# Gated delta rule: block-row sweeps written in place, four heads in four 32-column strips, and a new slot order

## What is computed

```
q, k, v = silu(conv4(x @ W))         # 128 channels a head, causal depthwise convolution of 4 taps
a, b    = sigmoid(x @ Wa + ba), sigmoid(x @ Wb + bb)
for t in range(256):
    err = S @ k_t - v_t
    S   = a_t * S - b_t * outer(err, k_t)
    o_t = S @ q_t
out = (layernorm(o) * sigmoid(x @ Wg)) @ Wo
```

## Time and profile before

| | |
|---|---|
| median of 3 runs | 3551.97 us (3543.28 to 3555.49) |
| profiled execution, its own time | 3545.73 us |
| span of its instructions | 3543.7 us |
| PE / DVE / ACT / POOL busy in the span | 89% / 70% / 53% / 52% |
| slots 10 to 63 | about us 1042 to 3060 of the span |
| draining slots and the second routed layer | from us 3094 |

### The profile page before, as it was taken

How to read it: one execution, slowest core, us unless ns; L and a number is a source line. 1 busy time by engine, 2 the same in 40 slices (tenths; PEclk the granted TensorE clock), 3 DMA queues, 4 the chain that set the end, 5 groups by cost and what they waited for, 6 DMA issues and landing times.

```text
span 3543.7 us, 68472 instructions
## 1 busy us (share of the span) xinstructions
PE 3137.7 (89%) x19888; PEld 2721.2 (77%) x19888; DVE 2494.0 (70%) x5733; ACT 1894.1 (53%) x3788; POOL 1829.4 (52%) x1918
## 2 busy tenths in 40 slices
PE   5999999646679999999999999999999999876773
PEld 3777777524469999899899899989989999766762
DVE  4565556565467778778777777777777777677766
ACT  2555555324356666666566566666656666433421
POOL 1111111133666767667576676766767676564332
PEclk9999999867799999999999999999999999988985
DMA  2000000023466565665656556566565665423211
GB/s 87 1 0 0 0 0 0 3 71 104 122 186 183 162 173 169 170 178 163 175 154 183 171 153 196 138 183 182 156 179 160 176 178 161 138 76 90 80 31 48
DMA packets 572226, 423.68 MB, mean 120 GB/s; under 512 B 228692, under 2 KB 475220, under 8 KB 571735
## 3 DMA queue, kind: packets, MB, share of 16 engines
q1 hardware_dynamic: 571862, 419.51, 41.6%
HBM read 276.39 MB, written 143.01 MB: 118 GB/s over the span
## 4 chain that ended last, share of the span: by engine, by line
PE 76%; DVE 13%; issue 4%; ACT 4%; POOL 3%; DMA 1%; DVEq 0%; SPq 0%; ACTq 0%; POOLq 0%
PE bank L1820 23%; PE bank L1871 22%; PE bank L1851 6%; PE bank L1955 5%; PE bank L1670 4%; PE bank L1645 3%; PE bank L1583 3%; PE bank L1655 2%; DVE dec L1427 1%; DVE acc L1418 1%; PE bank L1859 1%; POOL acc L740 1%; PE bank L1640 1%; ACT acc L972 1%; PE bank L1945 1%
## 5 line engine op out<-in xcount | busy, mean ns | idle before, releaser
L740 POOL TENSOR_TENSOR acc<-acc,shifted 128x510 f32<-128x510 f32 x384 | 611.2, 1594 | 448.6 <-DVE acc L1418 441.5
L1418 DVE SCALAR_TENSOR_TENSOR acc<-bank,conv_w,acc 128x254 f32<-128x254 f32 (+1 forms) x1536 | 631.0, 473 | 177.5 <-ACT acc L972 176.9
L970 ACT ACTIVATE shifted<-bank,conv_w 128x255 f32<-128x255 f32 x768 | 362.9, 472 | 435.4 <-PE bank L1820 310.7
L1820 PE MATMUL bank<-x_k,w_kq 128*128 128x256 f32 x2048 | 489.7, 384 | 41.9 <-DVE acc L1418 16.5
L1820 PEld LDWEIGHTS bank<-x_k,w_kq 128*128 128x128 f32 x2048 | 374.9, 192 | 92.1 <-issue 30.0
L972 ACT ACTIVATE acc<-bank,conv_b,conv_w 128x256 f32<-128x256 f32 x768 | 433.9, 565 | 0.0
L1871 PE MATMUL bank<-y,GT 128*128 128x128 f32 x2048 | 285.2, 284 | 56.5 <-DVE y L1458 56.5
L1871 PEld LDWEIGHTS bank<-y,GT 128*128 128x128 f32 x2048 | 269.9, 200 | 64.6 <-DVE y L1458 58.5
L1851 PE MATMUL bank<-kq 128*128 128x256 f32 x1024 | 276.1, 409 | 37.3 <-ACT kq L982 30.8
L767 POOL TENSOR_TENSOR ors<-ovar,half_neg 128x8 f32<-128x8 f32 x64 | 163.4, 2554 | 264.1 <-DVE ovar L1493 264.0
L757 POOL TENSOR_TENSOR inv<-inv,outer 128x30 f32<-128x30 f32 (+14 forms) x480 | 277.2, 578 | 37.6
(11 more groups left out here) (237 smaller groups left out, 6779.3 us busy)
## 6 DMA issues: line engine op xcount, KB each, us to landing
abc<-decay_scratch SPq DMA_DIRECT2D x64, 512.0 KB, 4.2
q_scratch<-kq SPq DMA_DIRECT2D x64, 512.0 KB, 3.8
M_scratch<-LM SPq DMA_DIRECT2D x64, 512.0 KB, 3.6
L_scratch<-LM SPq DMA_DIRECT2D x64, 512.0 KB, 4.8
LTm<-L_scratch SPq DMA_DIRECT2D x64, 512.0 KB, 4.1
MTm<-M_scratch SPq DMA_DIRECT2D x128, 256.0 KB, 3.6
kqm<-q_scratch SPq DMA_DIRECT2D x64, 512.0 KB, 4.2
k_scratch<-knw SPq DMA_DIRECT2D x64, 258.0 KB, 4.7
```

Of the source, the lines that this page charges most:

```text
L740: pool.tensor_tensor(dst, dst, shifted[:, u % 2, :, 1:], ALU.add).then_inc(Z["sumk" if u < 4 else "sumv"], 1)
L970: act.activation(shifted[:, u % 2, i % 2, 1:], pj[:, 0:SEQ - 1], ACT.Copy, scale=conv_w[:, kind, bass.ds(head, 1), TAPS - 2:TAPS - 1].rear ...
L1418: dve.scalar_tensor_tensor(out=acc[:, kind, i, t:], in0=pj[:, 0:SEQ - t], scalar=wcol, in1=acc[:, kind, i, t:], op0=ALU.mult, op1=ALU.add) ...
L1820: mm = pe.matmul(dst[:, i * SEQ:(i + 1) * SEQ], w[:, k, head * DK:(head + 1) * DK], x[:, k, :], start=(k == 0), stop=(k == CT - 1))
```

## The change

1. `GT` is filled once with identity matrices. `off_blocks` on DVE no longer multiplies by a mask but copies, for q = 32, 64, 96, the rows above block q into the block column q of `GT` (three copies of 32, 64 and 96 partitions x 4 heads x 32). The mask `above` is gone.
2. A sweep computes only block row k+1: `block_row` issues one matmul per head with a weight of 128x32 (the columns of that block of `GT`) and writes head i to partitions 32i to 32i+31 of the bank, so the four heads use the four 32-column strips of the PE array. Because of the identity in `GT` the product is already the finished row. It is copied in place into `vn` or `r1`: DVE copies heads 0 and 1, ACT copies heads 2 and 3 (32x128 each), and the next sweep waits for both (`y0` and `z0`, `y1` and `z1`). `y0`, `y1` are gone; the updates read `vn`, `r1`.
3. The order of the calls in a slot is new on all five engines, and two uses in `RING` change places. On DVE, `second_rhs` now stands before `decays` and `products`. On SP, `store_n` now stands before nine other transfers instead of last. On ACT, `silu(0)` stands before `tap(3)`.
4. In the preparation two pairs of store semaphores are merged, which changes no order.

The preparation on GpSimd:

```diff
+            pool.tensor_copy(GT[:].rearrange("p c h t -> p (c h t)"), id_many[:].rearrange("p n t -> p (n t)")).then_inc(Z["cons"], 1)
```

ScalarE's half of a sweep, new (`second_sweep` alike, with `r1`, `ap1`, `z1`):

```diff
+                def first_sweep(k):
+                    act.wait_ge(Z["ap0"], past(3 * h + k + 1))
+                    q = (k + 1) * BLK
+                    for i in range(HG // 2, HG):
+                        ins = act.copy(vn[hp][q:q + BLK, 0, i], bank[3][i * BLK:(i + 1) * BLK, 0:DK])
+                    ins.then_inc(Z["z0"], 1)
```

VectorE:

```diff
-                    dve.tensor_tensor(GT[:, tc], above[:].unsqueeze(1).broadcast_to([P, HG, P]), bank[3 + tc][:].rearrange("p (h t) -> p h t", h=HG),
-                                      ALU.mult).then_inc(Z["Gev"], 1)
+                    product = bank[3 + tc][:].rearrange("p (h t) -> p h t", h=HG)
+                    for q in range(BLK, P, BLK):
+                        ins = dve.tensor_copy(GT[0:q, tc, :, q:q + BLK], product[0:q, :, q:q + BLK])
+                    ins.then_inc(Z["Gev"], 1)
...
-                    dve.tensor_tensor(y0[:], vn[hp][:, 0], bank[3][:].rearrange("p (h v) -> p h v", h=HG), ALU.add).then_inc(Z["y0"], 1)
+                    q = (k + 1) * BLK
+                    for i in range(HG // 2):
+                        ins = dve.tensor_copy(vn[hp][q:q + BLK, 0, i], bank[3][i * BLK:(i + 1) * BLK, 0:DK])
+                    ins.then_inc(Z["y0"], 1)
```

TensorE:

```diff
+                def block_row(dst, lhsT, rhs, q, signal):
+                    for i in range(HG):
+                        mm = pe.matmul(dst[i * BLK:(i + 1) * BLK, 0:DK], lhsT[:, i, q * BLK:(q + 1) * BLK], rhs[:, i], start=True, stop=True)
+                    mm.then_inc(signal, 1)
...
-                    heads(bank[3], GT[:, 0], y0 if k else vn[hp][:, 0], Z["ap0"])
+                        pe.wait_ge(Z["z0"], past(3 * h + k))
+                    block_row(bank[3], GT[:, 0], vn[hp][:, 0], k + 1, Z["ap0"])
```

More of the change, by code:

```diff
@@ L562, in store_n @@
                     sp.dma_start(k_dram[p], knw[:]).then_inc(Z["st_n"], 16)
+                if hn is not None:
+                    load_l()
                 if ph == 0:
@@ L567, in slot @@
                     load_xk()
+                if p is not None:
+                    store_q()
                 if hn is not None:
-                    load_l(), load_xg(), load_m0()
+                    load_bn()
+                if p is not None:
+                    store_n()
+                if hn is not None:
+                    load_n()
+                if nn is not None:
+                    load_b1()
+                if hn is not None:
+                    load_m0()
                 if fn is not None:
@@ L1001, in keys, with second_sweep @@
                     act.copy(knw[:, 0:HG * DK], bank[ring_bank("kT", 0)][:]).then_inc(Z["kn"], 1)
+                def first_sweep(k):
[4 more added lines that the diff above has]
+                    ins.then_inc(Z["z0"], 1)
+                def second_sweep(k):
+                    act.wait_ge(Z["ap1"], past(3 * n + k + 1))
+                    q = (k + 1) * BLK
+                    for i in range(HG // 2, HG):
+                        ins = act.copy(r1[q:q + BLK, i], bank[5][i * BLK:(i + 1) * BLK, 0:DK])
+                    ins.then_inc(Z["z1"], 1)
                 def updates(c):
@@ L1043, in slot @@
                 if h is not None:
-                    updates(0)
+                    first_sweep(2), gate(0)
+                if p is not None:
+                    tap(3)
                 if f is not None:
                     tap(4)
-                if p is not None:
-                    silu(1)
+                if h is not None:
+                    gate(1), updates(0)
                 if f is not None:
@@ L1052, in slot @@
                     state()
+                if p is not None:
+                    silu(1)
                 if n is not None:
-                    affine(0), affine(1)
+                    affine(0)
                 if p is not None:
                     keys()
+                if n is not None:
+                    affine(1)
+                if h is not None:
+                    first_out(), from_state()
                 if f is not None:
@@ L1508, in slot @@
                 routed(0)
+                if n is not None:
+                    second_sweep(1)
+                if h is not None:
+                    off_blocks(0)
                 if p is not None:
                     conv(0)
+                if n is not None:
+                    second_sweep(2)
                 if h is not None:
-                    off_blocks(0)
-                if n is not None:
-                    second_sweep(1)
+                    first_sweep(0)
                 if p is not None:
                     conv(1)
-                if h is not None:
-                    first_sweep(0)
-                if n is not None:
-                    second_sweep(2)
-                if p is not None:
-                    conv(2)
                 if h is not None:
@@ L1542, in slot @@
                     normalise()
+                if h is not None:
+                    weighted()
+                routed(2)
                 if f is not None:
                     conv(4), conv(5)
-                if p is not None:
-                    decays(), products(0), products(1), products(2), products(3)
                 if h is not None:
@@ L1550, in slot @@
                 routed(4)
+                if p is not None:
+                    decays(), products(0), products(1), products(2), products(3)
                 if n is not None:
@@ L1983, in slot @@
                     second_out()
+                if middle:
+                    proj_g(0), first_sweep(2)
                 if pre:
```

153 lines of the change are left out of this document (72 added, 81 removed).

## The result

The changed kernel takes 3682.73 us (median of 4, 3672.37 to 3687.58) against 3552.49 us (3543.28 to 3555.49) for the kernel before on the same chip: ratio 1.0368 (95% interval 1.0345 to 1.039), slower by 3.7%. The forecast was 3525, in a range from 3455 to 3600.

The account below looks back on a forecast made before the run. PE's stream bounds slots 10 to 63 at 36.9 us; after the change SP's loop to MTm gives 36.6. 54 slots -16, ends -11, together -27: 3519 from the profiled 3545.7, or 3525 for the median, range 3455 to 3600.

Parts of the forecast that it names:

- rival 2: At second_out: load_m1 late from slow issuing and a full queue, slot 37.9 us in the middle, 3595 in all; chance 0.22.
- (a): On PE, from the start of second_out to the start of keys_on_state: 16.0 us.
- (b): On DVE, second_rhs, then scan and small copy, bringing the loop from second_out to 22.2 us.
- (c): SP's issuing: kqm issued at 29.0 us (31.1 at worst) after second_out, MTm three single transfers of 0.65 later.
- (d): Landing of MTm after second_out: 34.8 us at best, 36.7 with a full queue, 38.8 with slow issuing; 36.0 taken.
- the drain: Slots 64 to 73, PE at a mixed clock and waiting in turn with DVE: -15 us in all (0 to -30).
- the ends: Slots outside 10 to 63: -15 us in slots 64 to 73, +4 in slots 0 to 7, together -11.
- The sweep: On PE, four 128x32 products in strips: 0.70 us instead of 0.89, bounds 0.4 and 1.1, records strictly in order.
- Rival 4: On PE, all four strips run at once, 0.4 us a sweep, PE's slot 34.0, 3505 in all; chance 0.08.
- Nothing of PE comes within 1 us of POOL: POOL's pieces change places, but with 9 us of slack a slot they were expected not to hold PE.
- Rival 1: MTm's transfers are in time, so PE's 35.8 us slot holds: 3482 for the median; chance 0.20.
- rival 3: On PE, the strips don't overlap, 1.05 us a sweep, PE's slot 37.9: 3605 in all; chance 0.12.

Follow-up runs that it names:

- e15: Changed kernel with the load of MTm's second half directly behind kqm, ahead of x_g and abc in SP's queue: 3559.28 us, ratio 1.0018.
- e14: Changed kernel with the four small BDT loads moved from ahead of kqm to behind the load of MTm's second half: 3610.32 us, ratio 1.0158.
- e13: Changed kernel with DVE's decays (scan and weights copy) ahead of the second right-hand side again, MTm still late in SP's queue: 3611.31 us, ratio 1.017.
- e6: e1 with DVE's scan of the decays ahead of the second right-hand side again: 3522.76 us, ratio 0.9923.
- e5: e1 with the four heads of a sweep in two strips of the array instead of four: 3588.6 us, ratio 1.0119.
- e11: e4 with DVE and ACT copying the last block row of r ahead of the first block row of vn: 3467.28 us, ratio 0.9763.
- e1: Changed kernel with one transfer moved: load_m1 ahead of load_bn and store_n in SP's queue: 3543.84 us, ratio 0.999.
- e4: Block rows, copies and semaphores as in the changed kernel, but every engine's order as in the kernel before: 3495.59 us, ratio 0.9849.

## Why the prediction was wrong

The place and the mechanism were those of the text: PE idles ahead of the second-chunk U,MTm, the loop closes through `store_n`, DVE's scan and SP's queue. That is rival 2, which had 0.22; the forecast had taken the same loop 3 us shorter. Its steps, from U,MTm at 2025.24 to the next at 2065.10 (the last column leaves out what the steps before had added):

| step | predicted | measured | its own error |
|---|---|---|---|
| (a) to the start of keys_on_state | 16.0 | 17.55 | +1.55 |
| (b) to k_scratch | 22.2 | 23.95 | +0.2 |
| (c) issue of MTm | 30.95 | 32.60 | -0.1 |
| (d) landing | 36.0 taken (34.8 to 38.8) | 39.86 | +2.2 |

- **(d) is the term that failed.** I took 5.05 us after issue, between landing alone (3.8) and a full queue from kqm on (5.75, the value that the earlier trace rows gave). Measured: 6.5 in the median, and 7.3 to PE's start in this slot. e15 and e14 show the cause: two loads of 0.75 MB directly in front. The reasoning by bytes in the queue had named the right place; taking the middle with an empty queue was wrong, since the order itself puts four large loads within 1.8 us, and even the full queue was priced too low.
- **(a) left out what a wait does to PE.** U,MTm took 0.95 and x_g 0.66 us longer than at full speed, 1.61 in all; beside that the sweep was 0.34 shorter than taken and small edges 0.28 longer. So the loop feeds on itself: the wait lowers the clock, which lengthens the path to the next load. The row of the drain had shown this, and I used it for the drain alone. An estimate from these rows shows that the two terms are enough: 54 x (6.5 - 5.05) brings 3525 to 3603, and 54 x 1.55 more to 3687, against 3683 measured. That it is so close is in part luck, since PE didn't wait in every slot (38 waits in some 45).
- **(b), (c)** held to 0.2 us. e13 shows that they are on the path: take the scan out of (b) and the time falls by 71 us, where the same edit gave 21 in e6, with MTm in time.
- **The price of rival 2** was the middle of its case, +1.0 a slot; its far end, 39.4, would have given 54 x 2.5 = 135 us in the slots, or 3676 with the ends. Measured: 150 in the slots of the profiled execution, and a median of 3683. Rival 2 should have been priced across its span, and the range should have reached there.
- **The sweep**: taken 0.70, bounds 0.4 and 1.1, which hold the result. Measured 0.35 to the next start, 0.24 where two follow each other (2018.71 to 2018.95), and 0.1 at each edge (the next x_k lasts 1.83 and not 1.73): 0.55. The reading "strictly in order, 5 record times" fell; eight records in 0.24 us are two record times. The rows of attention had allowed this reading too: fully side by side they are 8 x 0.111 + 0.2 = 1.09 and 4 x 0.216 + 0.2 = 1.06, and I took the other one. Rival 4 had the mechanism right (its 0.4 is as far from 0.55 as my 0.70), and it didn't matter here, for the reason it gave. The Trainium skill (TensorE: Matmul & The Clock Gate, Part 3) says that packed tiles run side by side and a pack lasts about one matmul. The traces agree: 0.24 us with four strips, and 0.46 (2132.30 to 2132.76) with e5's two. The Trainium skill (TensorEngine Tiling (Array Packing), Key Properties) says that a change of the tiling mode drains the engine. The 0.1 us at each edge would fit that; no run here separates what it consists of.
- **PE's own work**: forecast 35.8 a slot. e11's usual slot is 35.5 with 0.48 of waits in it, so 35.0.
- **"Nothing of PE comes within 1 us of POOL" failed.** The order puts DVE's scan beside POOL's gating: 48.6 us of wait, 1.1 a slot, shown by e6. With the wait for S (e1: 45.7 us) it eats what the block rows save even where MTm is in time. In the changed kernel itself this wait costs little: PE waits 2.6 to 3.1 us for MTm behind it. Rival 1, "the transfers are in time, 3482", is therefore e1, and it took 3544.
- **Small terms.** DVE and ACT: pairs of copies 0.58 and 0.53 us (284 and 257 ns each) against 0.5 taken; ACT +191 us over the run where 3 us a slot meant 192. **The ends**: the drain was taken at -15, and the time behind the last slot is 15 shorter. The slots 0 to 7 were taken at +4, for `tap(3)` behind `silu(0)`; they are 2 us shorter (198.1 against 200.3), so that cost is not there.
- **Two sums of the rivals** don't add up as printed: rival 3 comes to 3611 by its own terms, not 3605, and rival 4 with rival 1 to 3380, not 3400. Neither changes a conclusion.

Open are: why the kernels with the new order take 41 to 49 us in every eighth slot (49 in e13), where e4 takes 40; what makes MTm's landing late, the bytes or the number of packets in front; and the new order with the old place of L's store.

## What to carry to other kernels

Where the order itself has put large loads directly in front of a load, price it from the issue of the first of them and not from its own (here it was 9.0 us from kqm's issue to PE's start). When a wait of PE is possible, add to the loop what the lower clock costs after it. A change of arithmetic and a new order should be timed apart: here the one gave 1.5% in the old order (2.4% with two copies exchanged), and the other lost 5%.

## What the runs showed of the hardware

- A GpSimd product of 128x512 takes 2.3 us beside VectorE's scan (e1) and 1.4 us where the scan stands ahead of it (e6).
- Four 128x32 products in four strips of the array: eight float32 records in 0.24 us where another such group follows, 0.35 with the change of shape behind them. In two strips: 0.46 and 0.57. Full-width ones: 0.89.
- Behind 3 us without work PE ran its next 4.5 us at a granted clock of 0.62 (2065.0 to 2069.5), where the stretch behind it stood at 1.00 (2070 to 2080).
- A load of 256 KB landed 4.1 us after its issue with one load of 512 KB directly ahead of it, and 6.5 us with 0.75 MB more between them (medians of e15 and of the changed kernel).
